# Routed attention stages: keys fetched during the top-k search, first queries in the routing block, scatter matrix last in a step, 128-row key fetches

## The reference

```
NQ, NK, H, DH = (128, 64, 8, 64)                     # g = 4 routers
q_top, q_idx = top_k(einsum('bnd,gd->bgn', x, w_qr), NQ)
kv_top, kv_idx = top_k(einsum('bnd,gd->bgn', x, w_kvr), NK)
q  = einsum('bgnd,ged->bgne', x[bidx, q_idx], w_q)
kv = einsum('bgnd,ged->bgne', x[bidx, kv_idx], w_kv);  k, v = split(kv)
v = v * sigmoid(kv_top);  k, v = concat([null_k, k]), concat([null_v, v])
o = softmax(q k^T * DH ** -0.5) v;  o = (o @ w_out) * sigmoid(q_top)
meaned = zeros.at[b, q_idx].add(o) / counts;  out = where(counts > 0, meaned, null_token)
```

## Time and profile before

| | |
|---|---|
| median of 3 runs | 3176.83 us (3171.78 to 3183.02) |
| profiled execution | 3183.64 us, its span 3181.9 us |
| granted TensorE clock, mean | 0.949 |
| busy | PE 2753.0 (87%), DVE 1912.5 (60%), ACT 1394.7 (44%), POOL 1099.9 (35%) |

### The profile page before, as it was taken

The page is one execution under the profiler, slowest core; times in us unless marked ns, Lnnn a source line. Parts: engine busy times, 40 slices in busy tenths (PEclk is TensorE's granted clock), DMA queues, the critical chain, the costliest instruction groups (busy, mean ns, idle before and its releaser), DMA issues. The chain is left out here.

```text
span 3181.9 us, 61905 instructions
## 1 busy us (share of the span) xinstructions
PE 2753.0 (87%) x24099; PEld 1784.3 (56%) x24131; DVE 1912.5 (60%) x4327; ACT 1394.7 (44%) x2896; POOL 1099.9 (35%) x1448
## 2 busy tenths in 40 slices
PE   7999599878699877787888799987999989799997
PEld 2343367656366655565555567764666556456664
DVE  7988454456454466734674566665666646466664
ACT  5655144434244334422453354443555534345553
POOL 4888344223344223312112333330222246212222
PEclk9899699999899988879999899999999999999999
DMA  2000200011000001110101000002222201112221
GB/s 79 1 1 1 77 14 15 5 25 28 23 15 15 5 1 41 38 61 17 30 22 30 16 1 1 1 3 72 66 69 71 68 18 32 57 43 73 81 66 46
DMA packets 62495, 105.48 MB, mean 33 GB/s; under 512 B 8138, under 2 KB 47062, under 8 KB 61440
## 3 DMA queue, kind: packets, MB, share of 16 engines
q1 hardware_dynamic: 56832, 94.63, 10.0%
q0 software_dynamic: 5376, 6.90, 0.8%
HBM read 78.09 MB, written 23.86 MB: 32 GB/s over the span
## 5 line engine op out<-in xcount | busy, mean ns | idle before, releaser
L566 ACT ACTIVATE s_sT<-s_R 128x1024 f32<-128x1024 f32 (+2 forms) x448 | 400.1, 945 | 199.4 <-PE s_R L500 198.5
L601 DVE TENSOR_REDUCE s_negm<-s_R 128x4 f32<-128x1024 f32 x320 | 377.0, 1220 | 156.3 <-PE s_R L471 156.2
L471 PE MATMUL s_R<-s_qk 32*128 32x256 f32 (+2 forms) x3584 | 241.8, 383 | 60.8 <-ACT s_sT L566 32.8
L500 PE MATMUL s_R<-s_qA,s_qk 32*128 32x256 f32 (+2 forms) x3584 | 240.6, 382 | 18.3 <-DVE s_negm L601 11.7
L573 ACT ACTIVATE s_oc<-s_OB 128x256 f32<-128x256 f32 x224 | 86.1, 384 | 342.8 <-PE s_OB L519 342.8
L519 PE MATMUL s_OB<-s_sT,s_v 128*32 128x256 f32 (+2 forms) x3584 | 226.2, 370 | 9.9 <-ACT s_sT L566 6.4
L471 PEld LDWEIGHTS s_R<-s_qk 32*128 32x128 f32 x3584 | 153.9, 185 | 108.8 <-issue 79.0
L616 DVE TENSOR_TENSOR s_qA<-s_qk,s_X 128x256 f32<-128x256 f32 x224 | 94.3, 421 | 194.9 <-PE s_X L531 194.9
L500 PEld LDWEIGHTS s_R<-s_qA,s_qk 32*128 32x128 f32 x3584 | 162.6, 185 | 79.5 <-issue 65.4
L1511 POOL TENSOR_TENSOR s_pr<-s_pr,s_rinv 128x1024 f32<-128x1024 f32 x64 | 121.3, 1895 | 218.9 <-DVE s_rinv L1621 218.9
L1593 ACT ACTIVATE s_pr<-s_S,s_negmax 128x256 f32<-128x256 f32 x256 | 118.7, 471 | 135.3 <-DVE s_negmax L1624 135.3
(11 more groups left out here) (588 smaller groups left out, 6248.0 us busy)
## 6 DMA issues: line engine op xcount, KB each, us to landing
s_wB<-enc_b SPq DMA_DIRECT2D x32, 962.5 KB, 4.7
s_scratch<-s_pk SPq DMA_DIRECT2D x58, 256.0 KB, 2.0
s_qk<-s_scratch SPq DMA_DIRECT2D x232, 64.0 KB
s_wA<-enc_a SPq DMA_DIRECT2D x32, 193.0 KB, 4.0
big<-moe SPq DMA_DIRECT2D x2, 2347.0 KB, 11.1
all_W<-weights SPq DMA_DIRECT2D x2, 2199.5 KB, 12.8
big<-routed SPq DMA_DIRECT2D x2, 2084.0 KB
s_returned<-s_back SPq DMA_DIRECT2D x2, 1024.0 KB
```

The lines of the kernel that those rows point to most:

```text
L471: last = pe.matmul(S[h][:, t * T:t * T + hi - lo], b.qk[rows, r % 2, 0, c, t * P:(t + 1) * P], b.qk[rows, r % 2, 1, c, lo:hi], start=(t == ...
L500: last = pe.matmul(b.R[:, a.turned_at(u, h // 2), :][:, h % 2, a.at(kt)], b.qk[rows, r % 2, 1, c, kt * P:(kt + 1) * P], b.qA[rows, u % 2, ...
L566: act.activation(b.sT[:, u % (a.lag + 1), 2 * p:2 * p + 2, 0:a.width], b.R[:, a.turned_at(u, p), 0:a.width], ACT.Exp).then_inc(s.expd, 1)
L601: ins = dve.tensor_reduce(b.negm[:, u % 2, :, at].rearrange("p t h -> p h t"), S.rearrange("p h (t k) -> p h t k", t=TT), AX_X, ALU.max, n ...
```

## The change

Routing block: after the eighth search step the positions found so far are converted, transposed and turned into `first_kv`, the row numbers of the keys; GpSimd waits for them and issues the key fetches of the first eight units while the search goes on. `index` is computed right behind the search, ahead of the mask and no longer behind the sigmoid, and GpSimd issues the query fetches of the first four units in this block too. Attention block: group 0 takes keys, k, queries, q in this order, with four dummy matmuls ahead of each query transpose; later key fetches (units 8 to 31) bring 128 rows instead of 64, all of which are transposed and 64 used; `place_rows(i)` stands at the end of VectorE's step; a one-column exponential is ScalarE's first instruction. What the softmax, projections and scatter compute is the same.

```diff
-                items += self.front(0, "gather") + self.front(0, "q") + self.front(0, "k")
+                items += [("keys", 0)] + self.front(0, "k") + [("queries", 0)] + self.front(0, "q")
...
+    def gathered(self, u):
+        group = u // self.NB
+        return self.number[("gather", group, u % self.NB // 2) if group else ("queries", 0)] + 1
...
+        first_kv = st.sb("first_kv", [NK, ROWS], mybir.dt.uint32)
+        hq = st.sb("hq", [P, 2 * NB, D])
+        hk = st.sb("hk", [P, 2 * NB, D])
...
+        def fetch_queries(pool, u):
+            c, ring = columns(u)[0], u % (2 * NB)
+            pool.indirect_dma_start(hq[:, ring, :], None, sent, bass.IndirectOffsetOnAxis(index[:, c:c + 1], 0),
+                                    bounds_check=NTOK - 1, oob_is_err=False).then_inc(got_q[ring], 16)
+        def key_rows(u):
+            return NK if u < 2 * NB else P
+        def fetch_keys(pool, u):
+            c, ring, n = columns(u)[1], u % (2 * NB), key_rows(u)
+            at = first_kv if u < 2 * NB else index
+            pool.indirect_dma_start(hk[0:n, ring, :], None, sent, bass.IndirectOffsetOnAxis(at[0:n, c:c + 1], 0),
+                                    bounds_check=NTOK - 1, oob_is_err=False).then_inc(got_k[ring], 16)
...
+                    pool.wait_ge(stored, 32 if have else 16)
+                    pool.wait_ge(half_index, 1)
+                    for u in range(2 * NB):
+                        fetch_keys(pool, u)
+                    pool.wait_ge(index_ready, 1)
+                    for u in range(NB):
+                        fetch_queries(pool, u)
...
-                    pe.wait_ge(steps, 35)
+                    pe.wait_ge(half_found, 1)
+                    pe.transpose(ST[0:NK, 2 * ROWS:3 * ROWS], found_f[:, 0:NK], g.ident[0:ROWS, 0:ROWS])\
+                      .then_inc(half_back, 1)
+                    pe.wait_ge(steps, 36)
                     keep_busy(pe, g, HT[:, 0, :], 16)
+                    pe.wait_ge(sorted_, 1)
+                    pe.transpose(ST[:, 0:ROWS], found_f[:], g.ident[0:ROWS, 0:ROWS]).then_inc(back, 1)
...
+                        if 8 * (k + 1) == NK:
+                            dve.tensor_copy(found_f[:, 0:NK], found[:, 0:NK]).then_inc(half_found, 1)
+                        if 8 * k == NK:
+                            dve.wait_ge(half_back, 1)
+                            d.done(dve.tensor_copy(place_kv[:], ST[0:NK, 2 * ROWS:3 * ROWS]))
+                            dve.tensor_tensor(first_kv[:], place_kv[:], g.w("r_first")[0:NK, :], ALU.add)\
+                               .then_inc(half_index, 1)
...
+                    dve.wait_ge(back, 1)
+                    d.done(dve.tensor_copy(place[:], ST[:, 0:ROWS]))
+                    dve.tensor_tensor(index[:], place[:], g.w("r_first"), ALU.add).then_inc(index_ready, 1)
                     dve.tensor_tensor(mask[:], work[:, 0, :], row[:], ALU.not_equal).then_inc(mask_ready, 1)
-                    dve.wait_ge(sig_ready, 1)
-                    d.done(dve.tensor_copy(place[:], ST[:, 0:ROWS]))
-                    d.mark(dve.tensor_tensor(index[:], place[:], g.w("r_first"), ALU.add))
...
+                        if it[0] == "keys":
+                            for u in range(NB):
+                                pe.wait_ge(got_k[u], 16)
+                                last = pe.transpose(f[:, u * NK:(u + 1) * NK], hk[0:NK, u, :], g.ident[0:NK, 0:NK])
+                        elif it[0] == "queries":
+                            for u in range(NB):
+                                keep_busy(pe, g, OUT[:], 4)
+                                pe.wait_ge(got_q[u], 16)
+                                last = pe.transpose(f[:, u * NQ:(u + 1) * NQ], hq[:, u, :], g.ident[:])
...
-                                last = pe.transpose(f[:, at + NQ:at + NQ + NK], hk[:, ring, :],
-                                                    g.ident[0:NK, 0:NK])
+                                last = pe.transpose(f[:, at + NQ:at + NQ + n], hk[0:n, ring, :], g.ident[0:n, 0:n])
...
+                    act.activation(warm[:], sig[:, 0, 0:1], ACT.Exp)
...
                     null_keys(0)
                     for u in range(NB, 2 * NB):
-                        fetch(u)
+                        fetch_queries(pool, u)
...
                         if i + 2 * NB < U:
-                            fetch(i + 2 * NB)
+                            pool.wait_ge(f_mm, plan.gathered(i))
+                            fetch_queries(pool, i + 2 * NB)
+                            fetch_keys(pool, i + 2 * NB)
...
                                               ALU.subtract).then_inc(shifted, 1)
-                            place_rows(i)
                             dve.wait_ge(expd, i + 1)
...
                                                          op0=ALU.mult, op1=ALU.add).then_inc(added, 1)
+                        if i < U:
+                            place_rows(i)
                         if i - 2 in left:
```

More of the change, by code:

```diff
@@ L2956, in routed_attention_stage, with columns @@
         nw = st.sb("nw", [H, 4, D])
+        first_kv = st.sb("first_kv", [NK, ROWS], mybir.dt.uint32)
+        hq = st.sb("hq", [P, 2 * NB, D])
+        hk = st.sb("hk", [P, 2 * NB, D])
+        got_q = [st.sem(f"got_q{k}") for k in range(2 * NB)]
+        got_k = [st.sem(f"got_k{k}") for k in range(2 * NB)]
+        def columns(u):
+            s, b = plan.unit(u)
+            return b * 2 * G + s, b * 2 * G + G + s
+        def fetch_queries(pool, u):
[9 more added lines that the diff above has]
+                                    bounds_check=NTOK - 1, oob_is_err=False).then_inc(got_k[ring], 16)
         with Stage(nc, name + "r") as sr:
@@ L3121, in routed_attention_stage @@
                                     "projected", "o_cp", "scattered", "added", "nulled")]
[L3123 to L3129, removed]
             def copied(*item):
@@ L3155, in item @@
                             s = plan.unit(group * NB)[0]
-                            pe.wait_ge(f_cp, copied("gather", group, 1))
+                            pe.wait_ge(f_cp, copied("gather", group, 1) if group else copied("queries", 0))
                             last = pe.matmul(f, wq[:, (4 * s + c) * P:(4 * s + c + 1) * P], sel[:, group % 2, :, 0:NQ],
@@ L3161, in item @@
                             s = plan.unit(group * NB)[0]
+                            if group == 0:
+                                pe.wait_ge(f_cp, copied("keys", 0))
                             for c in (2 * k, 2 * k + 1):
@@ L3253, in _ @@
                             act.wait_ge(f_mm, n + 1)
-                            if it[0] == "gather":
+                            if it[0] == "keys":
+                                act.activation(sel[:, 0, :, NQ:NQ + NK],
+                                               f[:, 0:NB * NK].rearrange("p (b s) -> p b s", b=NB), ACT.Copy)\
+                                   .then_inc(f_cp, 1)
+                            elif it[0] == "queries":
+                                act.activation(sel[:, 0, :, 0:NQ], f.rearrange("p (b s) -> p b s", b=NB), ACT.Copy)\
+                                   .then_inc(f_cp, 1)
+                            elif it[0] == "gather":
                                 _, group, k = it
                                 act.activation(sel[:, group % 2, 2 * k:2 * k + 2, :],
-                                               f[:, 0:2 * (NQ + NK)].rearrange("p (b s) -> p b s", b=2), ACT.Copy)\
+                                               f.rearrange("p (b s) -> p b s", b=2)[:, :, 0:NQ + NK], ACT.Copy)\
                                    .then_inc(f_cp, 1)
@@ L3298, in null_keys @@
                             .then_inc(nullk, 1)
-                    def fetch(u):
-                        ring = u % (2 * NB)
-                        q, k = columns(u)
-                        if u >= 2 * NB:
-                            before = u - 2 * NB
-                            pool.wait_ge(f_mm, plan.number[("gather", before // NB, before % NB // 2)] + 1)
-                        pool.indirect_dma_start(hq[:, ring, :], None, sent,
-                                                bass.IndirectOffsetOnAxis(index[:, q:q + 1], 0),
-                                                bounds_check=NTOK - 1, oob_is_err=False).then_inc(got_q[ring], 16)
-                        pool.indirect_dma_start(hk[:, ring, :], None, sent,
-                                                bass.IndirectOffsetOnAxis(index[0:NK, k:k + 1], 0),
-                                                bounds_check=NTOK - 1, oob_is_err=False).then_inc(got_k[ring], 16)
-                    for u in range(NB):
-                        fetch(u)
                     null_keys(0)
                     for u in range(NB, 2 * NB):
-                        fetch(u)
+                        fetch_queries(pool, u)
                     for i in range(U + plan.TAIL):
```

26 lines of the change are left out of this document (13 added, 13 removed).

## The result

The changed kernel takes 3139.65 us in the median of four runs (3135.71 to 3144.99), beside 3177.31 for the kernel before in its four: a ratio of 0.988, with a 95% interval of 0.986 to 0.991. The forecast was 3152 with a range of 3142 to 3165, so the kernel is faster than the range allows. The direction came as forecast; the gain was 37.7 us where the sum said 25.0. The profiled execution has a span of 3138.0 us.

A forecast was written before the change was run, and what follows sets the result against it. TensorE was taken to set the pace, idling at the turn and the start. 20.0 + 3.4 + 0.5 - 3.0 + 4.1 = 25.0 us takes the median from 3176.83 to about 3152, range 3142 to 3165.

The forecast's parts named there:

- The turn: Attention steps: TensorE no longer waits for s3a_pn once place_rows comes last; nine waits of 1.10 us per stage, 20.0 in all.
- The last unit's wait: Step 31: result comes 1.0 us after TensorE wants it, against 2.72 before; 1.7 gained per stage, 3.4 in all.
- the 0.8 us put down to the moments of the layer-norm: Steps 29 to 31: four small VectorE instructions for the next stage, between scatter matrix and maximum, eat most of the margin.
- The clock in the tail of s3: After s3's long last wait: a shorter wait may keep TensorE's clock up, about 1 us once, 0.5 counted.
- The wider keys: Gather steps: 128-row key transposes cost 0.26 instead of 0.20 us; 1.5 us slower per stage, -3.0 in the sum.
- The start: Search to first scores: earlier fetches gain 1.3 us in s3, 2.8 in s1; together 4.1, bounds 0 and 8.
- rival (b): The start gives nothing or loses, 0 to -3 us per stage; time 3156 to 3162 us; chance 0.20.
- rival (a): Fetches don't get through during the search, start 9.1 us later per stage; time 3170 us; chance 0.06.
- the Trainium skill's trap: Search fetches: VectorE holding the shared port blocks GpSimd's descriptors; start 14 us later per stage, time near that before.
- The change of block took 0.8 us: Routing to attention block: 0.8 us from the end of the dummies to the next, so TensorE starts at 859.0.
- rival (d): GpSimd's issues slow down beside VectorE and bound the steps; slower, 24 us per stage, about 3221 us; chance 0.02.
- Rival (c): TensorE still waits at the turn, ScalarE's copy of v being as late; time 3172 to 3176 us; chance 0.04.

The follow-up runs named there:

- the run of that part alone: The kernel before with only place_rows(i) moved to the end of VectorE's step: 3153.47 beside 3182.92 us, ratio 0.990.
- the kernel with the outer semaphores: The kernel before with only hq, hk and their sixteen semaphores declared in the outer scope: 3186.81 beside 3184.38 us, ratio 1.0014.
- the start alone: The changed kernel with 64-row key fetches and place_rows(i) back in its old place: 3182.01 beside 3182.92 us, ratio 0.9993.

## Why the prediction was right in its direction and wrong in its size

**The turn: right.** Forecast 20.0 + 3.4 us, measured 21.1 + 4.2; the run of that part alone shows it, mechanism and size. The short step came out at 5.42, not 5.50. The last unit's wait fell from 2.72 to 0.60 rather than to 1.0; the 0.8 us put down to the moments of the layer-norm was probably too much. The clock in the tail of s3 gave 1.4, forecast 0.5, with "about 1 us once" as its full size.

**The wider keys: the step that failed.** "Keys of 128 rows cost 0.06 more in 24 units" read two distances of the earlier trace rows, 0.26 and 0.20, as the prices of a large and a small transpose. They were mostly the prices of two changes of row count. The term has the wrong sign: +7.4 us for -3.0, and 10.4 of the 13.0 us between forecast and result come from it. The 4.5 us that the start fell short and the 4.3 us in the rows of the first four steps and of the change of block, which the sum had at nothing, cancel by luck. "I see nothing that the wider fetch gives back" looked at the fetch, and the gain was on TensorE. The trace before the change had the row that contradicts the price by size, two rows further down in the same kind of step:

```profile
910.54 0.27 PE L3151 MATMUL s3a_F<-all_ident,s3a_hk 64*128 64x64 f32 x1
910.74 0.27 PE L3177 MATMUL s3a_F<-all_ident,s3a_pn 128*8 128x128 f32 x1
910.85 0.60 PE L3206 MATMUL s3a_PT<-all_ident,s3a_pr 128*128 128x128 f32 x4
911.38 0.33 PE L3218 MATMUL s3a_OT<-s3a_prT,s3a_v 64*64 64x128 f32 x2
```

One transpose of 128 rows 0.11 us ahead of the next, and four with the step down to 64 rows behind them in 0.53, can't each cost 0.26. Asking why one of the same shape took 0.26 elsewhere would have given the term.

**The start: rival (b), held at 0.20.** The search grew by 0.5 us (0.65 forecast), the eight key fetches took 0.94 us each beside MAX8 and MATCH_REPLACE8 (938 to 1213 ns, median 943), and rival (a) falls. The fetches also did not meet the Trainium skill's trap (SBUF — State Buffer, "DVE blocks DMA"); its condition is a two-port operation of VectorE, and whether the search instructions are such, no run here shows. Of (b) the start came true, not its 3156 to 3162, since the wider keys went the other way. What failed is mainly one number. "The change of block took 0.8 us" holds where TensorE's dummies end last; behind GpSimd's last issue it took 2.9 us (841.63 to 844.5). With the first query issued 1.9 us after the search instead of 1.1, TensorE started 9.7 us after it, where the forecast has 859.0 - 851.75 = 7.25: 2.4 us per stage, 0.7 of it from the later first issue, 4.9 in all, which covers the 4.5 missing. From there to the first scores the sum said 16.2 and the trace says 16.1. A last fetch needs 2.6 us from issue to landing, and 840.63 + 2.6 + 1.2 gives 844.4; that the block waits for the landing is argued from this and was not tested.

**GpSimd as the bound: rival (d) falls.** The issues took 992 to 1083 ns for queries and 997 to 1020 for keys of 128 rows.

**Rival (c) falls**: the waits are gone.

**Not foreseen.** The first four steps took 24.0 us in both stages of the changed kernel for 24.75 and 25.4 before. Its second profile has 23.4 and 24.0, while the kernel with the outer semaphores, which starts as the one before, has 24.7 and 25.8 and the start alone 25.0 twice. So the 2.1 us are more than chance in one profile. They go with where the lower level of the clock falls in these steps; what places it there was not tested. The 2.2 us behind the stage go with the start part; by what, stays open: the semaphores' scope was ruled out, the instruction count of the block and the wait of GpSimd were not tried. Search, start, first four steps and change of block together are +3.9 us in the first profile of the changed kernel and -0.3 in that of the start alone, whose medians give 0.9 with an interval that holds zero.

## What to carry to other kernels

Read the price of a matmul from rows with the same neighbour as well as the same shape: a distance between two rows also pays for what has to change between them, and padding an operand to the shape of its neighbour, or grouping equal shapes, can be cheaper than the smaller work. An issue moved ahead of a barrier hides only if the barrier has something later to wait for: the four query fetches ahead of it cost 3 to 4.5 us of start a stage and were better behind it. Filler matmuls that stand in order ahead of real work cost their time whenever the data is already there; without them the next projection ran at the lower clock in one stage of four, so weigh the one against the other. Profile a kernel twice before giving a difference of some tenths of a microsecond a cause: two profiles of the changed kernel differ by up to 0.12 us in the same gather step and by 1.1 us in the same start.

## What the runs showed of the hardware that was not expected

- At 2.4 GHz fp32 transposes of 128 rows settle at a start every 0.11 us and those of 64 rows at one every 0.07. From one row count to the other it is 0.16 to 0.21 us, and the distance behind such a change is 0.05 us longer than usual; in turn, 128 to 64 takes 0.26 and 64 to 128 takes 0.20.
- The change of block takes 0.8 to 1.2 us behind TensorE's dummies and 2.9 to 3.0 us behind GpSimd's last indirect fetch.
- Five dummies take 1.24 us after an idle time of 0.8 or 1.2 us in some stages and 2.29 us after 0.84 us in others. The level of the eight dummies ahead doesn't settle which: 1.24 us was seen behind eight in 1.90 and behind eight in 3.59, 2.29 us behind eight in 2.72 and in 3.60. After 4.7 us of idle time they took 2.29 in the changed kernel.
